# The power of a row normalisation, asked for in two parts

## The reference

```python
def _layernorm(x, axis=-1, eps=1e-05):
    m = jnp.mean(x, axis=axis, keepdims=True)
    v = jnp.var(x, axis=axis, keepdims=True)
    return (x - m) / jnp.sqrt(v + eps)

x = x + _L0_gnn_ref(_layernorm(x), edge_index, ...)
x = x + _L0_ffn_ref(_layernorm(x)[None], ...)[0]
...
x = x + _L3_gnn_ref(_layernorm(x), edge_index, ...)
x = x + _L3_ffn_ref(_layernorm(x)[None], ...)[0]
```

## Time and profile before

| | us |
|---|---|
| three timed runs | 1747.12, 1747.79, 1752.88 |
| their median | 1747.79 |
| the profiled execution | 1743.42 |
| its span, first to last instruction | 1741.6 |
| PE busy | 1624.4 (93%), 8683 instructions |
| DVE busy | 1251.1 (72%), 2075 |
| ACT busy | 936.4 (54%), 1590 |
| POOL busy | 246.9 (14%), 250 |
| TensorE's granted clock, mean | 0.97 of full speed |

### The profile page before, as it was taken

How to read it: one execution, slowest core, us unless ns; L and a number is a source line. 1 busy time by engine, 2 the same in 40 slices (tenths; PEclk the granted TensorE clock), 3 DMA queues, 4 the chain that set the end, 5 groups by cost and what they waited for, 6 DMA issues and landing times. The chain is left out here.

```text
span 1741.6 us, 26178 instructions
## 1 busy us (share of the span) xinstructions
PE 1624.4 (93%) x8683; PEld 1264.3 (73%) x8683; DVE 1251.1 (72%) x2075; ACT 936.4 (54%) x1590; POOL 246.9 (14%) x250
## 2 busy tenths in 40 slices
PE   7779899999998999888999989898899999999998
PEld 6657666687885787556888856585578888888886
DVE  7873764246574466569999967444589999999998
ACT  1122345433461355126999825431267877888874
POOL 2200553001120012023000030100081000000003
PEclk9889898899999999989999999999999999999999
DMA  9001000003101001214784140002325608945003
GB/s 308 31 0 49 1 1 1 13 1 134 50 2 37 1 1 62 97 59 152 250 316 138 36 162 1 0 1 87 131 75 232 241 18 361 365 202 235 18 24 95
DMA packets 42464, 173.60 MB, mean 100 GB/s; under 512 B 10220, under 2 KB 10473, under 8 KB 26906
## 3 DMA queue, kind: packets, MB, share of 16 engines
q1 hardware_dynamic: 28822, 153.94, 23.5%
q0 software_dynamic: 8960, 10.29, 2.2%
q10 hardware_dynamic: 4608, 8.39, 1.3%
HBM read 275.74 MB, written 19.51 MB: 170 GB/s over the span
## 5 line engine op out<-in xcount | busy, mean ns | idle before, releaser
L665 POOL DMA_INDIRECT sb_W<-slots_out,sb_slus x20 | 28.1, 1404 | 606.2 <-DMA slots_out<-sb_rC 600.8
L1413 ACT ACTIVATE sb_rF<-sb_rF,sb_nmx 125x625 f32<-125x625 f32 (+4 forms) x120 | 89.5, 746 | 44.9 <-DVE sb_nmx L1911 44.9
L747 PE MATMUL bank<-sb_ones 128*128 128x512 f32 x224 | 102.8, 607 | 7.8 <-DVE sb_rC L2411 6.3
L357 DVE TENSOR_TENSOR sb_rA_r<-sb_W,sb_rA_r 128x1024 fp32r<-128x1024 f32 x68 | 83.5, 1228 | 11.9 <-ACT sb_rA_r L1512 11.7
L614 POOL TENSOR_TENSOR sb_rstd<-sb_ve,sb_half 125x5 f32<-125x5 f32 (+1 forms) x17 | 18.9, 1114 | 506.5 <-DVE sb_ve L1832 248.6
L1911 DVE CUSTOM_DVE_ANT_0 sb_rF<-bank,sb_rG 125x625 f32<-125x625 f32 x80 | 61.5, 807 | 36.0 <-PE bank L839 35.2
L747 PEld LDWEIGHTS bank<-sb_ones 128*128 128x128 f32 x224 | 42.1, 194 | 57.2 <-issue 49.1
L357 DVE TENSOR_TENSOR sb_rB_r<-sb_W,sb_rB_r 128x1024 fp32r<-128x1024 f32 x68 | 83.2, 1223 | 0.0
L357 DVE TENSOR_TENSOR sb_XT_r<-sb_W,sb_XT_r 128x1024 fp32r<-128x1024 f32 x68 | 83.0, 1221 | 0.0
L1136 PE MATMUL bank<-sb_rA 125*125 125x313 bf16 x400 | 61.6, 319 | 21.2 <-DVE sb_rA L2237 18.0
L1512 ACT ACTIVATE sb_rA_r<-sb_W 128x1024 fp32r<-128x1024 f32 x68 | 71.4, 1051 | 17.4 <-DMA sb_W<-in_w_m 14.8
(11 more groups left out here) (499 smaller groups left out, 4878.3 us busy)
## 6 DMA issues: line engine op xcount, KB each, us to landing
sb_W<-in_w_m SPq DMA_DIRECT2D x204, 1024.0 KB
sb_rDE<-in_w_m SPq DMA_DIRECT2D x17, 1024.0 KB
sb_rC<-slots_in SPq DMA_DIRECT2D x34, 256.0 KB, 3.4
sb_W<-in_w_g SPq DMA_DIRECT2D x8, 1024.0 KB, 5.0
slots_out<-sb_rC ACTq DMA_DIRECT2D x32, 256.0 KB, 2.0
slots_in<-sb_rC SPq DMA_DIRECT2D x1, 4608.0 KB, 14.5
sb_W<-in_w_a SPq DMA_DIRECT2D x4, 1024.0 KB, 30.6
sb_W<-in_w_m SPq DMA_DIRECT2D x2, 2048.0 KB, 18.7
```

The costliest lines, as they stand in the source:

```text
L357: eng.tensor_tensor(lo, src[:, HALF * h:HALF * (h + 1)], hi.bitcast(F32), ALU.subtract).then_inc(split(r, p, h, b, "lo")[0], 1)
L665: pool.indirect_dma_start(out=G[r][k][:, t], out_offset=None, in_=YS[0:P * KEPT], in_offset=bass.IndirectOffsetOnAxis(ap=slus[:, k, t:t + ...
L747: pe.matmul(bank[:, b, :], ones[:], ones[:, 0:1].broadcast_to([P, D]), start=True, stop=True)
L1413: act.activation(SM[:, s % 4, 0:kn], SM[:, s % 4, 0:kn], ACT.Exp, scale=-1.0, bias=nmx[:, s:s + 1], accum_out=dens[:, s:s + 1]).then_inc(S ...
```

## The change

`moments` is called behind each tile's statistics and does something behind two of them. Behind tile 2 it waits, aggregates tiles 0 to 2 and adds epsilon to three variances; behind tile 4 it does the same for tiles 3 and 4. GpSimd takes two powers, of three columns and of two, each when its variances are there. `normalise` waits for the first power ahead of tile 0 and for the second ahead of tile 3. So a norm has 17 counted instructions on VectorE instead of 16, and two powers instead of one; the tables and the counts that other engines wait for are moved to match. ln2's power stays one of five columns, and ln1's own code still waits for both powers before it goes on.

```diff
-        NORMS = 6 + 2 * T + 2 * LAYERS
-        POW = {"ln0": 1, "bn0": 2, "ln1": 3, "ln2": 4, ...}
-        LN = [16 * k if k < 2 else 16 * (k - 1) + 4 for k in range(9)]
+        NORMS = 9 + 2 * T + 2 * LAYERS
+        POW = {"ln0": 2, "bn0": 3, "ln1": 5, "ln2": 6, ...}
+        EARLY = 3
+        LN = [17 * k if k < 2 else 17 * (k - 1) + 4 for k in range(9)]
...
             def ln(k):
-                power(rstd3[:] if k == 2 else rstd[0:R, :], ve[0:R, :], T, S("ln_vec"), LN[k] + 11 if k != 2 else LN[1] + 14)
+                if k == 2:
+                    power(rstd3[:], ve[0:R, :], T, S("ln_vec"), LN[1] + 15)
+                else:
+                    power(rstd[0:R, 0:EARLY], ve[0:R, 0:EARLY], EARLY, S("ln_vec"), LN[k] + 2 * EARLY + 1)
+                    power(rstd[0:R, EARLY:T], ve[0:R, EARLY:T], T - EARLY, S("ln_vec"), LN[k] + 2 * T + 2)
...
                     c(dve.bn_stats(st[0:R, t], src(t)))
-                moments(c)
-
-            def moments(c):
-
-                for t in range(T):
-                    if t == 0:
-                        c.sync()
-                    c(dve.bn_aggr(mv[0:R, t], st[0:R, t]))
-                c.sync()
-                c(dve.tensor_scalar(ve[0:R, :], mv[0:R, :, 1], EPS, None, ALU.add))
+                    moments(c, t)
+
+            def moments(c, t):
+
+                if t not in (EARLY - 1, T - 1):
+                    return
+                a, b = (0, EARLY) if t == EARLY - 1 else (EARLY, T)
+                c.sync()
+                for i in range(a, b):
+                    c(dve.bn_aggr(mv[0:R, i], st[0:R, i]))
+                c.sync()
+                c(dve.tensor_scalar(ve[0:R, a:b], mv[0:R, a:b, 1], EPS, None, ALU.add))
...
             def normalise(c, k, src):
-                dve.wait_ge(S("pow"), POW[f"ln{k}"])
                 for t in range(T):
+                    if t in (0, EARLY):
+                        dve.wait_ge(S("pow"), POW[f"ln{k}"] - (t == 0))
                     c(dve.tensor_scalar(XN[:, t], src[:, t], mv[0:R, t, 0:1], rstd[0:R, t:t + 1], ALU.subtract, ALU.mult))
...
                     n(dve.bn_stats(st[0:R, t - 1], X[:, t - 1]))
-            moments(n)
+                    moments(n, t - 1)
             normalise(n, 4, X)
...
                     n(dve.bn_stats(st[0:R, i - 2], X[:, i - 2]))
-            moments(n)
+                    moments(n, i - 2)
             normalise(n, 6, X)
```

More of the change, by code:

```diff
@@ L409, in graph_network @@
         CONSTS = 24
-        NORMS = 6 + 2 * T + 2 * LAYERS
-        POW = {"ln0": 1, "bn0": 2, "ln1": 3, "ln2": 4, "degr": 5, "q": 6, "k": 6 + T, "ln3": 6 + 2 * T, "lf": NORMS + 1, "ln4": NORMS + 2,
-               "ln5": NORMS + 3, "l2": NORMS + 4, "ln6": NORMS + 5, "ln7": NORMS + 6, "bn3": NORMS + 7, "ln8": NORMS + 8}
-        LN = [16 * k if k < 2 else 16 * (k - 1) + 4 for k in range(9)]
+        NORMS = 9 + 2 * T + 2 * LAYERS
+        POW = {"ln0": 2, "bn0": 3, "ln1": 5, "ln2": 6, "degr": 7, "q": 8, "k": 8 + T, "ln3": 9 + 2 * T, "lf": NORMS + 1, "ln4": NORMS + 3,
+               "ln5": NORMS + 5, "l2": NORMS + 6, "ln6": NORMS + 8, "ln7": NORMS + 10, "bn3": NORMS + 11, "ln8": NORMS + 13}
+        EARLY = 3
+        LN = [17 * k if k < 2 else 17 * (k - 1) + 4 for k in range(9)]
         RT_ACT = {0: 0, 1: 9, 2: 14, 3: 23}
@@ L634, in scatter @@
             def scatter(r):
-                pool.wait_ge(S("ln_vec"), LN[4 if r == 1 else 8] + 16)
+                pool.wait_ge(S("ln_vec"), LN[4 if r == 1 else 8] + 17)
                 pool.wait_ge(S("sl_vec"), SLOT_OPS * (r // 2) + 9)
@@ L702, in _ @@
             ln(3)
-            pool.wait_ge(S("ln_vec"), LN[3] + 16)
+            pool.wait_ge(S("ln_vec"), LN[3] + 17)
             pool.wait_ge(S("ld_rvec"), 16)
@@ L749, in ln_to_feats @@
             def ln_to_feats(k, behind=None):
-                to_feats(XN, S("tr_full"), S("ln_vec"), LN[k] + 11 if k != 2 else LN[1] + 15, 1, behind)
+                to_feats(XN, S("tr_full"), S("ln_vec"), LN[k] + 12 if k != 2 else LN[1] + 16, 1, behind)
             def streamed(dst, gains, xt, i, done):
@@ L2267, in _ @@
             assert edges.n == EDGE_PREP + 6
-            normalise(Chain(dve, S("ln_vec"), LN[0] + 11), 0, X)
-            dve.wait_ge(S("ln_vec"), LN[0] + 16)
+            normalise(Chain(dve, S("ln_vec"), LN[0] + 12), 0, X)
+            dve.wait_ge(S("ln_vec"), LN[0] + 17)
             add_norm(0)
@@ L2528, in _ @@
             feats(8, XT)
-            dve.wait_ge(S("ln_vec"), LN[7] + 16)
+            dve.wait_ge(S("ln_vec"), LN[7] + 17)
             add_norm(2 * T)
```

## The result

The changed kernel takes 1737.01 us in the median of its runs (1731.11 to 1748.30), the kernel before 1747.05 (1741.92 to 1752.93, 20 runs beside them). One run of the changed kernel, at 2925.56 us with a granted clock of 0.77, is left out. The profiled execution took 1736.99 us, its span is 1735.2. The forecast was 1740.0.

A forecast was written before the change was run, and what follows sets the result against it. Bound: serial row norms, VectorE idle 7.7 us for GpSimd's power. Direct terms 2 x 0.98 + 3 x 1.00 + 1.3 - 0.56 = 5.7, less 0.1, plus clock 2.0: 7.6 off 1747.79 gives 1740; range 1734.5 to 1746.5.

The forecast's parts named there:

- the clock's 5 us: Upper bound of the gain from TensorE's granted clock; 2.0 us was taken, the lower bound was -2.
- The costs of the pieces: Estimated us: power of three columns 0.85, of two 0.70; aggregation of three tiles 0.31, of two 0.25.
- One norm: Net direct saving per norm: 0.98 us in ln3 and ln7, 1.00 in ln4, ln6 and ln8, 1.3 in ln5.
- The 0.1 for ln8's fillers: In ln8 TensorE's fillers end just when the first tile would be ready; 0.1 us taken off the saving.
- delay of 0.56: In ln1 early aggregations hold up the additions TensorE waits for; loss taken as 0.56 us, between nothing and 0.6.
- The clock: Shorter idle keeps norm transposes at full clock: 1.6 us in ln5, 1.8 for ln4 and ln7; 2.0 of 3.4 taken.
- 1.6 us gained: In ln5, idle falls to 0.9 us, so its transposes should stay at full clock and gain 1.6 us.
- Port: GpSimd's powers beside VectorE: cost taken 0; second power some 0.2 us late, perhaps again at its write, within 0.5 spare.
- Rivals 1 and 3: In six norms VectorE held up: by the second power, 0.70 us each (chance 0.14); by both, 1.55 each, slower (0.04).
- Rival 4: Early power not early, or tile order makes the second late: only ln1's loss remains, 1748 us; chance 0.04.
- The base: The time the saving was taken from: the median of three timed runs of the kernel before, 1747.79 us.
- the direct sum: Direct savings of the norms less ln1's loss, 5.7 us, less 0.1 in ln8: 5.6 us.

The follow-up runs named there:

- e9: Changed kernel with more TensorE fillers ahead of ln4, ln6 and ln7, plus fillers in three places around ln1; 1731.33 us, ratio to before 0.9919.
- e10: As e9, but in ln3 to ln8 the early aggregations stand behind tile 3's statistics instead of tile 2's; 1731.32 us, ratio to before 0.992.
- e4: Changed kernel with more TensorE fillers: two more ahead of ln4 and ln7, one more ahead of ln6; 1734.05 us, ratio to before 0.9933.
- e11: Kernel before, nothing split, with one unused 640-column VectorE instruction delaying ln1 behind tile 2's statistics; median 1746.54 us, ratio 0.9987.

## Why the prediction was right, and where its sizes were off

For the six norms its mechanism held step by step; for ln1 and for the clock it did not. The time of 1740.0 was 3 us above the 1737.0 measured, and its nearness is luck in part. The sum with all of the clock's 5 us ends at 1747.79 - 5.6 - 5 = 1737.2; the range went 2.7 us below that, to 1734.5, with no row for the difference, and the measured time lies just inside that piece.

- *The costs of the pieces.* Power of three columns 0.85 (0.85 measured, but 1.22 to 1.32 in ln4, ln5 and ln6), of two 0.70 (0.70 in ln0 and ln1), three aggregations 0.31 (0.31), two 0.25 (0.25). The line through the powers of 4, 5 and 8 columns in the earlier trace rows holds down to one column, which took 0.56 with one tile early.
- *One norm.* 0.98 to 1.00 expected, 1.01 to 1.02 measured; ln5 1.3 and 1.30, but that is of this pair of traces: the same stretch took 14.86 to 15.25 us in five traces that leave ln5 alone, and 13.73 to 13.95 in four with the same split. The 0.1 for ln8's fillers did not come: they were not in the way.
- *ln1.* Its delay of 0.56 was measured at 0.55, and what it was to cost was wrong in sign. The step that failed is "the delay of 0.56 is not [hidden]": it took the rest of the stage as fixed in length. The small matmuls and ln2's transposes got 2.7 us shorter by the clock, and the next stretch 4.2. The prediction had said that ln1's longer idle could bring half clock to other places; in the traces it took half clock away.
- *The clock.* 2.0 was taken, bounds -2 to 5. The runs give 3.0 by one way and 4.6 by the other, and part of the 3.0 can be waits. For the norms' transposes the prediction worked out 3.4. They did get 3.1 shorter (ln5 1.6, ln4 and ln7 0.8 each), but what came through to the next matmul is 0.22 + 0.76 + 0.82 = 1.8: the term "1.6 us gained" for ln5 was mis-sized, since VectorE comes late to the copies there. Nor is the shorter idle shown to be the reason: ln5's transposes were at full clock after 1.54, 1.94, 2.37 and 2.46 us of idle in the four other traces that leave ln5 alone, and at half clock after 2.18 in before's. The rest of the clock's effect is outside the norms, in both signs, and there the prediction had no row.
- *Port.* Taken as 0 for VectorE and some 0.2 for the second power: it took 0.92 in all six norms, and the normalisations kept their 0.457. Rivals 1 and 3 had VectorE held up by 0.7 to 1.55 a norm. By the Trainium skill ("SBUF — State Buffer", Who interferes with whom) the port pair would be the power's for the whole instruction; this case's traces don't agree for a power. The two powers asked for at once show it best: there both lay between 401.37 and 402.88, VectorE's five normalisations started at 402.26, inside the second power, and took their 2.37 none the less. In the other direction a hold is seen: a power that starts inside a normalisation takes 0.92 for 0.70.
- *Rival 4* needed a late power; the spare times were 0.65 and 0.28, where 0.7 and 0.5 were worked out. The second is short by the 0.22 of the port.
- *The base.* The prediction took its saving from the median of three runs, 1747.79. The median of the 20 runs beside the changed kernel is 1747.05; 0.7 of the 3 us is that. Another 0.2 is the direct sum, 5.8 for 5.6; the rest is what the clock and the waits gave beyond 2.0.

What stays open: how often an execution takes the better course behind ln1, what in ln1's stretch decides it, and how the 3.0 us beyond the direct terms part into clock and waits. The idle alone does not: line 1191's transposes followed 1.54 us of idle in the changed kernel and 0.67 with the fillers of e9, and in both the clock stayed up through ln2's transposes; in the kernel before, after 0.98, it fell ahead of them.

## What to carry to other kernels

A wait between two engines in a short serial chain can be hidden by cutting the chain's input in two, if making the second part takes longer than the first part's round trip, and the second part's round trip fits under the work on the first: here 3 of 5 tiles, with 0.65 and 0.28 us to spare. With 4 the first condition failed in ln3 (0.12 of wait), with 1 the second (0.91); 2 was not run. Splitting only the producer cost 0.35 us a norm, and splitting only the power gave 0.32 of the 1.01. Where the clock of TensorE changes within the kernel, one profile on each side does not show what the clock is worth: count direct terms in the trace and leave the rest to the means of many runs. Before a rest is called the clock's, look for stretches at equal clock and for waits on DMA, and take the worth of a faster step at the next thing that waits for it.

## What the runs showed of the hardware

The runs of several kernels fall in groups, and the profiles of e9 and e10, which are the same up to ln3, fell one in each (1732.69 and 1741.46 us). They part within the first 60 us, in the first network. First e9: the timeline's row of 83 equal matmuls, and the window around them; then the same two of e10.

```profile
44.82 11.28 PE L1141 MATMUL bank<-sb_rA 125*125 125x313 bf16 x83 [2.81 <-DVE sb_rA L2247]
```

```profile
45.00:60.00 15.00, 14.08 (x104) 13.58 (x104) 13.55 (x45) 3.78 (x10) 0.00 (x0) 1.00 0.19 76
```

```profile
45.59 14.24 PE L1141 MATMUL bank<-sb_rA 125*125 125x313 bf16 x83 [2.81 <-DVE sb_rA L2247]
```

```profile
45.00:60.00 15.00, 14.24 (x83) 13.19 (x83) 12.52 (x39) 0.53 (x2) 0.43 (x1) 0.78 0.18 75
```

In e10's execution the clock was at 0.78 in that window, and its stretches to ln0's and ln2's transposes are 107.72 and 82.51 us long, where e9's are 103.08 and 76.96. These 10.2 us are more than the whole difference of the two spans (8.8). The profiles of e4 (1744.76 us) and e11 (1752.29) took the slower course too, with 107.67 and 107.88 us to ln0's transposes and a clock of 0.78 and 0.77 in that window; the other eleven have 102.6 to 104.9. Ahead of ln0's statistics, at some 80 us, all these kernels run the same instructions, and both e9 and e10 have runs near 1731 and near 1741.5, so the course does not seem to be set by the kernel. The Trainium skill ("TensorE: Matmul & The Clock Gate", Part 1: The HAM clock gate) says that the chip's watch on TensorE runs freely and does not start anew with the kernel, so that the same kernel can come out differently; these two traces agree in that the same matmuls took 11.28 and 14.24 us; the reason they do not show.

A power on GpSimd gets slower when it starts inside some instructions of VectorE, and none was seen to slow VectorE. In ln3 the one of two columns, started 0.17 into a normalisation, took 0.92 instead of 0.70; with the power split alone it started 0.07 before the normalisation and took 0.70. The one of three columns started 0.17 into a statistics instruction and took its 0.85. In ln4 the one of three took 1.28 instead of 0.85: it started at 740.34, 0.18 us into one of VectorE's additions with two inputs, and that addition took its usual time.

Its row in the changed kernel's timeline, and the addition's:

```profile
740.34 1.28 POOL L615 TENSOR_TENSOR sb_rstd<-sb_ve,sb_half 125x3 f32<-125x3 f32 x1 [6.18 <-DVE sb_ve L1839]
...
740.16 0.74 DVE L2455 SCALAR_TENSOR_TENSOR sb_X<-sb_XN,sb_rstd,sb_X 125x512 f32<-125x512 f32 x1
```
